# Cross-attention kernel on one core: the mask moved into the score product, and exp and clip over three score banks instead of two

## The chip, the cores and the metric

The kernel runs on one core of one Trainium2 chip. The metric is device time in microseconds from one launch; of three runs before the change the median is 766.37 us (765.65 to 770.05). Five engines work side by side and meet at semaphores: PE (TensorE, matmuls), ACT (ScalarE, activations), DVE (VectorE), POOL (GpSimd) and SP (SyncE, which here only issues DMAs).

## The reference, cut to what matters

Two blocks run one after the other over x (4 batches of 256 rows of 256) with a context of 1601 rows per batch. Block one is a one-head attention and a mixture of 16 experts. Block two is a 16-head attention over the same context, a layer norm of its result, and a second mixture of experts. The change concerns the 16-head attention (head size 16):

```
q, k, v = proj(hs, Wq, bq), proj(at, Wk, bk), proj(at, Wv, bv)
scores = clip(einsum('bhsd,bhtd->bhst', q, k) / 4, -50, 50)
scores = where(attend, scores, -10000.0)
scores = clip(scores, -50.0, 50.0)
probs  = softmax(scores, axis=-1)
probs  = probs / (probs.sum(axis=-1, keepdims=True) + 1e-08)
ctx    = einsum('bhst,bhtd->bhsd', probs, v)
```

A masked key has the score -50, so its weight is exp(-50) and not zero.

## The kernel before, in words

The program is one long hand-ordered instruction stream for each engine. Its parts in time are: block one's attention with the key and value projections of block two beside it (to about 200 us of the profile), the first mixture of experts (to about 430 us), the second attention (434.8 to 660.9 us), and the second mixture of experts with the routing. Only the second attention and the lines that prepare it are touched.

**Jobs and units.** The second attention has 16 jobs (`NJ`): 4 batches times 4 groups of 4 heads. A job has 13 key tiles (`MT`) of 128 keys, the last with 65. One key tile of one job is a unit, numbered x = 0 to 207 (`NALL`).

**Scores (`qk`, line 958).** A head's query and key have 16 numbers each. They are split in a high and a low part, and stand as 48 rows (`KR`): keys high, low, high against queries high, high, low. Two heads lie above each other in the partitions, at rows 0 to 47 (t = 0) and 64 to 111 (t = 1), so that a matmul of one and a matmul of the other use different row halves of the PE array. A unit has four such matmuls of 256 columns, (c, t) = (0,0), (0,1), (1,0), (1,1); the two of one t go to one PSUM bank of 512 columns. So a unit fills two banks, and six banks hold three units (`RING`).

**Exp (line 1438), on ACT.** One activation over the two banks of a unit, 1024 columns, into one of six buffers of `p32` (`PBUF`). The mask comes in as a bias: `kbias`, one number per key, which is a partition here, -1e30 for a masked key and 0 otherwise. Since keys are partitions and each unit has other keys, a bias column belongs to one unit only.

**Clip (line 1946), on DVE.** Clamps the 1024 columns between exp(-50) and exp(50) in place.

**Values (`pv`, line 1000).** For each of the 4 heads of the unit, a matmul with the 17 columns of values and a one (the softmax sum) as weights and 256 columns of `p32` in full fp32, which the profile shows as two MATMULs each. The four heads write to four column groups of the array. They accumulate over the job's 13 units in bank 6 or 7.

**Order on PE.** Line 1079: units go in pairs. First `qk(x)` and `qk(x+1)`, then for each of the two what else is due at that number (`early`: query projections and transposes for later batches; `between`: the output projection, the transposes and router logits of the batch before; `flip`: two transposes of a finished job's result), and then `pv(x-4)` and `pv(x-3)` (`PV_LAG` 4). `qk(x)` waits for `p_exp` of unit x-3, `pv(x)` for `p_clip` of unit x, exp of unit x for `pv_done` of unit x-6.

**Order on ACT and DVE.** Unit by unit, with the small work of `early` and `between` after the exp or clip of its number. On DVE, `evac(job-1)` (a copy of a finished job's result) comes after clip m = 3 and `norm(job-1)` after clip m = 5 of the next job; `flip` on PE is at m = 7 and waits for `evac`.

**SP.** `keys(job)` brings a job's keys to one of three slots of `kst` with six DMAs of 16 partitions. The first three jobs' keys and batch 0's values are asked for in a row; a later job's when the job three before it is scored.

Of the kernel before, what the change touches and what calls it, by code (L numbers as in the profile page):

```python
# [23 lines left out]
P = 128  # L24
# [31 lines left out]
KR = 3 * HD  # L56
PBUF = 6
RING = 3
KSL = 3
PV_LAG = 4  # L60
# [16 lines left out]
def build(nc, a, out, stop="D"):  # L77
    kh_d = nc.dram_tensor("k_hi", [NB * D, MP], F32).ap()
    kl_d = nc.dram_tensor("k_lo", [NB * D, MP], F32).ap()
    v_d = nc.dram_tensor("v_one", [NB, P, MT * NH * VW], F32).ap()  # L80
# [5 lines left out]
    with ExitStack() as ctx:  # L86
# [18 lines left out]
        keep = sb("keep", [P, NB * MT], I32)  # L105
        kbias = sb("kbias", [P, NB * MT])
# [27 lines left out]
        with ExitStack() as s:  # L134
# [20 lines left out]
            Bt("gap3b", [P, 2032])  # L155
# [6 lines left out]
        with ExitStack() as s:  # L162
            C = lambda name, shape, dt=F32: sbuf(s, name, shape, dt)
            qst = C("qst", [P, NB, NH // 2, SEQ], F32R)
            p32 = C("p32", [P, PBUF, 1024])
# [91 lines left out]
        keep_in, kbias_rdy = sem("keep_in"), sem("kbias_rdy")  # L257
# [40 lines left out]
        def at(x):  # L298

            return x // MT, x % MT  # L300

# [68 lines left out]
        def _(sp):  # L370
# [69 lines left out]
            sp.dma_start(keep[:], a["keep"]).then_inc(keep_in, 16)  # L440
# [33 lines left out]
            for t, s in ((wq_raw[:], a["wqT"].rearrange("(k p) n -> p k n", p=P)), (bq[:], a["bq"]),  # L474
# [4 lines left out]
                         (rs[:], a["rs"].rearrange("(o n) -> o n", o=1).broadcast_to([P, 1])), (bq0[:], a["bq0"])):  # L479
# [19 lines left out]

# [23 lines left out]

            for g in range(1, NG - 1):
                queries(0, g)
            for job in range(KSL, NJ):
                sp.wait_ge(sc_rdy, (job - KSL + 1) * MT)
# [133 lines left out]
        def _(pe):  # L661
# [244 lines left out]
            pe.wait_ge(cw_rdy, 6)  # L906
# [29 lines left out]
            def qk(x):  # L936

                job, m = at(x)
                b, g = job // NG, job % NG
                if m == 0:  # L940
                    pe.wait_ge(k_in[job % KSL], 96 * (job // KSL + 1))
                    if b == 0 and g == 0:
                        pe.wait_ge(q_lo, 4)
                    elif b == 0:
                        pe.wait_ge(q_in[g], 16 * 3 * HG)
                    elif b == 1 and g == 0:
                        pe.wait_ge(q_lo, 10)
                    elif b == 2 and g == 0:
                        pe.wait_ge(q_in[NG], 16 * 3 * HG * NG)
                if x >= RING:  # L950
                    pe.wait_ge(p_exp, x - RING + 1)
                elif x == 1:
                    pe.wait_ge(add_rdy, 4)
                rows = rows_of(m)
                for c in range(2):
                    for t in range(2):
                        r = slice(64 * t, 64 * t + KR)
                        mm = pe.matmul(ps[0:rows, 2 * (x % RING) + t, c * SEQ:(c + 1) * SEQ], kst[r, job % KSL, c, m * P:m * P + rows],  # L958
                                       qst[r, b, 2 * g + c, :], start=True, stop=True, skip_group_check=True)
# [25 lines left out]
            def pv(x):  # L985
# [9 lines left out]
                pe.wait_ge(p_clip, x + 1)  # L995
                rows = rows_of(m)
                for j in range(HG):
                    at_ = (m * NH + g * HG + j) * VW
                    c, t = j // 2, j % 2
                    mm = pe.matmul(ps[32 * j:32 * j + VW, 6 + job % 2, 0:SEQ], vsl[0:rows, b % 2, at_:at_ + VW],  # L1000
                                   p32[0:rows, x % PBUF, (2 * t + c) * SEQ:(2 * t + c + 1) * SEQ], start=m == 0, stop=m == MT - 1, skip_group_check=True)
# [76 lines left out]

            for x in range(0, NALL + PV_LAG, 2):
                for y in (x, x + 1):  # L1080
                    if y < NALL:
                        qk(y)
                for y in (x, x + 1):
# [4 lines left out]
                    if y >= PV_LAG:  # L1088
                        pv(y - PV_LAG)
# [1253 lines left out]
```

## Time and profile before

| | us |
|---|---|
| runs (three) | 765.65, 766.37, 770.05 |
| median | 766.37 |
| span of the profiled execution | 765.5 |
| second attention in it (434.8 to 660.9) | 226.1 |
| PE / ACT / DVE busy in the whole span | 702.9 / 396.4 / 537.3 |

The profiled execution's span of 765.5 us lies 0.2 us below the fastest run and 0.9 us below the median; the profile gives no other time for it. Busy PE in this profile counts modelled ends of overlapped matmuls, so 97% busy doesn't say that PE has no room. What it does is better read from the starts of its groups of matmuls: from the start of one group to the start of the next.

### The profile page before, as it was taken

The page shows a single profiled execution, that of the slowest core. Times are in us where ns is not written, and L with a number is a line of the kernel's source. Part 1 is how long each engine was busy: PE and PEld are TensorE (multiplying, and loading weights), DVE is VectorE, ACT ScalarE, POOL GpSimd, SP SyncE. Part 2 cuts the span into 40 slices and gives each one's busy share as a digit, 9 for nine tenths or more (in the row PEclk, how much of TensorE's full clock was granted, in tenths as well). Part 3 has the DMA queues.
Part 4 walks back from the last instruction along what each step waited for, and adds up shares of the span by engine and source line. Part 5 has one row for each costly group of instructions (what it writes and reads, how often), then busy time and mean ns, then how long its engine had stood idle before and what let it go on. Part 6 is the DMA issues. An engine that isn't in the chain of part 4 may idle for free.

```text
span 765.5 us, 14907 instructions
## 1 busy us (share of the span) xinstructions
PE 702.9 (92%) x5499; PEld 531.4 (69%) x5499; DVE 537.3 (70%) x1174; ACT 396.4 (52%) x564; POOL 174.1 (23%) x220
## 2 busy tenths in 40 slices
PE   4899989899899999999999699999999999998990
PEld 3688878798677888888888554455455454577880
DVE  6766566657486666666667788789888878776665
ACT  2633223243322323232322599999999999533550
POOL 5461514421001000000000050002302603532551
PEclk9999999999999999999999899999999999899996
DMA  7456375642625767776778949996969840464545
GB/s 245 132 172 232 122 263 175 221 166 87 186 78 195 248 209 235 253 234 206 237 253 136 192 74 142 209 136 102 210 109 186 128 71 2 133 268 126 166 127 191
DMA packets 55212, 131.16 MB, mean 171 GB/s; under 512 B 12160, under 2 KB 29952, under 8 KB 51568
## 3 DMA queue, kind: packets, MB, share of 16 engines
q1 hardware_dynamic: 51888, 122.93, 60.5%
q0 software_dynamic: 2256, 6.18, 2.4%
q10 hardware_dynamic: 1008, 1.25, 0.5%
q8 instruction: 38, 0.62, 0.4%
q14 instruction: 22, 0.18, 0.1%
HBM read 78.78 MB, written 48.79 MB: 167 GB/s over the span
## 4 chain that ended last, share of the span: by engine, by line
PE 55%; ACT 12%; issue 11%; DVE 9%; DMA 7%; POOL 4%; SPq 1%; DVEq 0%; POOLq 0%; ACTq 0%
PE ps L656 12%; PE ps L657 12%; PE ps L658 12%; ACT p L1438 8%; PE ps L1000 5%; PE ps L958 4%; PE ps L1188 4%; DMA raw<-in_ctxT 2%; PE ps L1204 2%; POOL cTl L612 2%; DMA raw<-in_ctxN 2%; DMA k_lo<-kl 1%; PE ps L1022 1%; ACT cNh L1267 1%; POOL cNl L599 1%
## 5 line engine op out<-in xcount | busy, mean ns | idle before, releaser
L1438 ACT ACTIVATE p<-ps,kbias 128x1024 f32<-128x1024 f32 (+1 forms) x208 | 211.3, 1163 | 5.2 <-PE ps L958 5.0
L1946 DVE TENSOR_SCALAR p<-p 128x1024 f32<-128x1024 f32 (+1 forms) x208 | 140.9, 689 | 26.1 <-ACT p L1438 24.5
L1000 PE MATMUL ps<-p,vsl 128*17 128x256 f32 (+1 forms) x1664 | 113.9, 383 | 2.0 <-DVE p L1946 1.0
L1343 ACT ACTIVATE hh<-h 128x512 fp32r<-128x512 f32 x50 | 31.6, 632 | 132.9 <-DVE h L1813 115.9
L958 PEld LDWEIGHTS ps<-qst,kst 48*128 48x128 f32 (+1 forms) x832 | 58.6, 182 | 60.2 <-ACT p L1438 32.7
L958 PE MATMUL ps<-qst,kst 48*128 48x256 f32 (+1 forms) x832 | 91.1, 318 | 5.5 <-ACT p L1438 1.5
L359 POOL TENSOR_SCALAR nv<-mv 128x2 f32<-128x2 f32 x8 | 6.2, 774 | 359.6 <-DVE mv L1876 211.8
L656 PE MATMUL ps<-xTh,w_hi 128*128 128x512 f32 x200 | 79.8, 399 | 1.5 <-DVE h L1809 0.8
L657 PE MATMUL ps<-xTl,w_hi 128*128 128x512 f32 x200 | 79.2, 396 | 0.0
L658 PE MATMUL ps<-xTh,w_lo 128*128 128x512 f32 x200 | 78.9, 394 | 0.0
L1000 PEld LDWEIGHTS ps<-p,vsl 128*17 128x17 f32 (+1 forms) x1664 | 35.9, 96 | 39.6 <-issue 7.1
L1815 DVE TENSOR_TENSOR hl<-h,hh 128x512 fp32r<-128x512 f32 x50 | 34.6, 692 | 36.6 <-ACT hh L1343 36.6
L656 PE MATMUL ps<-w_hi,hh 128*128 128x256 f32 x200 | 56.9, 284 | 2.1 <-DVE hl L1815 2.0
L1809 DVE TENSOR_TENSOR h<-silu,ps 128x512 f32<-128x512 f32 x50 | 34.4, 689 | 33.5 <-PE ps L658 22.4
L658 PE MATMUL ps<-w_hi,hl 128*128 128x256 f32 x200 | 56.6, 283 | 0.0
L657 PE MATMUL ps<-w_lo,hh 128*128 128x256 f32 x200 | 56.6, 283 | 0.0
L599 POOL TENSOR_TENSOR cNl<-raw,cNh 128x1024 fp32r<-128x1024 f32 (+1 forms) x16 | 31.4, 1983 | 78.1 <-ACT cNh L1267 78.1
L656 PEld LDWEIGHTS ps<-xTh,w_hi 128*128 128x128 f32 x200 | 37.7, 189 | 9.8 <-DVE h L1809 1.7
L658 PEld LDWEIGHTS ps<-xTh,w_lo 128*128 128x128 f32 x200 | 37.5, 187 | 9.0
L657 PEld LDWEIGHTS ps<-xTl,w_hi 128*128 128x128 f32 x200 | 37.8, 189 | 6.5
L656 PEld LDWEIGHTS ps<-w_hi,hh 128*128 128x128 f32 x200 | 38.1, 191 | 6.0 <-DVE hl L1815 4.0
L1339 ACT ACTIVATE silu<-ps 128x512 f32<-128x512 f32 x50 | 29.9, 597 | 19.9 <-PE ps L658 19.0
(308 smaller groups left out, 1551.3 us busy)
## 6 DMA issues: line engine op xcount, KB each, us to landing
x_slots<-blank SPq DMA_DIRECT2D x20, 1032.0 KB, 5.9
kst<-k_hi SPq DMA_DIRECT2D x64, 200.2 KB, 9.1
w_raw<-in_w SPq DMA_DIRECT2D x25, 384.0 KB, 3.5
v_one<-vst SPq DMA_DIRECT2D x4, 1768.0 KB, 8.9
vsl<-v_one SPq DMA_DIRECT2D x4, 1768.0 KB, 17.4
kst<-k_lo SPq DMA_DIRECT2D x32, 200.2 KB, 8.8
raw<-in_ctxN SPq DMA_DIRECT2D x12, 512.0 KB, 5.7
k_hi<-kh SPq DMA_DIRECT2D x24, 256.0 KB, 2.6
```

The costliest lines, as they stand in the source:

```text
L599: pool.tensor_tensor(cNl[:, c0:c0 + w, :], src, cNh[:, c0:c0 + w, :].bitcast(F32), ALU.subtract).then_inc(ctx_split, 1)
L656: e.matmul(o, lh, rh, start=first, stop=False, skip_group_check=True)
L657: e.matmul(o, lh, rl, start=False, stop=False, skip_group_check=True)
L658: return e.matmul(o, ll, rh, start=False, stop=last, skip_group_check=True)
L958: mm = pe.matmul(ps[0:rows, 2 * (x % RING) + t, c * SEQ:(c + 1) * SEQ], kst[r, job % KSL, c, m * P:m * P + rows], qst[r, b, 2 * g + c, :], ...
L1000: mm = pe.matmul(ps[32 * j:32 * j + VW, 6 + job % 2, 0:SEQ], vsl[0:rows, b % 2, at_:at_ + VW], p32[0:rows, x % PBUF, (2 * t + c) * SEQ:(2 ...
L1188: mm = pe.matmul(ps[:, 2 + j % 2, 0:2 * P], xbT[:, j % 2, k * P:(k + 1) * P], weights_of(j, slice(k * 2 * P, (k + 1) * 2 * P)), start=k == ...
L1343: act.activation(hh[:, half, :], h32[:, half, :], ACT.Copy).then_inc(hh_rdy, 1)
L1438: act.activation(p32[0:rows, x % PBUF, :], psf[0:rows, bank * 512:bank * 512 + 1024], ACT.Exp, scale=0.25, bias=kbias[0:rows, col:col + 1] ...
L1809: dve.tensor_tensor(h32[:, half, :], silu[:, half, :], ps[:, 5, :], ALU.mult).then_inc(mul1_rdy, 1)
L1815: dve.tensor_tensor(hl[:, half, :], h32[:, half, :], hh[:, half, :].bitcast(F32), ALU.subtract).then_inc(hl_rdy, 1)
L1946: dve.tensor_scalar(t, t, CLO, CHI, ALU.max, ALU.min).then_inc(p_clip, 1)
```

## The change

It does five things.

1. **Mask.** `keep`, `kbias` and the bias of the exp go. A 49th row joins the score product: in `kst` it holds 0 or -2^100 for each key (`bar_rows`, made by one DVE instruction and sent through DRAM), in `qst` it holds 1. The ones come from spare columns of the weights `wgh`/`wgl` (zeroed) and of the bias `bq0` for the queries that are computed in place, and from six DMAs for the others. `keys(job)` issues eight DMAs instead of six.
2. **Groups.** The 416 banks of scores (2 for each of 208 units) are taken three at a time, over the borders of units and jobs: 139 groups (`NGRP`), the last with two banks. Six banks of PSUM are two slots. `p32` has four buffers of 1536 columns, as many bytes as before.
3. **Exp and clip** are one instruction for each group, over 1536 columns and all 128 partitions, without a bias pointer.
4. **Order of the score product.** The six matmuls of a group go in the order (bank, c) = (0,0), (1,0), (2,0), (1,1), (0,1), (2,1). Banks 0 and 2 of a group have the same t.
5. **Order on PE.** One group of scores, then all other work due, then the values of the units that end in the group three before (`PV_LAG` 3): by turns two units and one.

```diff
-KR = 3 * HD
-PBUF = 6
-RING = 3
+KR = 3 * HD + 1
+BAR = -2.0 ** 100
+PBUF = 4
+GB = 3
+NBANK = 2 * NALL
+NGRP = -(-NBANK // GB)
 KSL = 3
-PV_LAG = 4
+PV_LAG = 3
...
+        def group_of(x):
+            return (2 * x + 1) // GB
+        def units_of(g):
+            return range(-(-(GB * g - 1) // 2), min((GB * g + GB - 2) // 2 + 1, NALL)) if 0 <= g < NGRP else range(0)
+        def width_of(g):
+            return 512 * min(GB, NBANK - GB * g)
...
             load_rest(FFN["B"])
+            sp.wait_ge(bar_rdy, 1)
+            sp.dma_start(bar_d, bar_f).then_inc(row_out, 16)
             scratch_out()
+            sp.wait_ge(row_out, 16)
...
+                    at_ = 64 * t + KR - 1
+                    sp.dma_start(kst[at_:at_ + 1, job % KSL, :, :].bitcast(F32), bar_d[job // NG:job // NG + 1, :].unsqueeze(1).broadcast_to([1, 2, MP])).then_inc(k_in[job % KSL], 16)
...
+            sp.wait_ge(q_hi, 1)
+            sp.wait_ge(tri_rdy, 1)
+            for t in range(2):
+                row = slice(64 * t + KR - 1, 64 * t + KR)
+                every = qst[row, :, :, :].rearrange("o b h (i n) -> o (b h i) n", n=P)
+                per = NH // 2 * SEQ // P
+                for lo, hi in ((4, per), (per + 4, 2 * per), (2 * per, NB * per)):
+                    sp.dma_start(every[:, lo:hi, :].bitcast(F32), ones[0:1, :].bitcast(F32).unsqueeze(1).broadcast_to([1, hi - lo, P])).then_inc(row_out, 16)
...
+            def qk(k):
+                banks = range(GB * k, min(GB * k + GB, NBANK))
+                for n in banks:
+                    if n % (2 * MT) == 0:
+                        first_of(n // (2 * MT))
+                if k >= 2:
+                    pe.wait_ge(p_exp, k - 1)
+                else:
+                    pe.wait_ge(add_rdy, 3 + k)
+                for i, c in ((0, 0), (1, 0), (2, 0), (1, 1), (0, 1), (2, 1)):
+                    if i < len(banks):
+                        x, t = banks[i] // 2, banks[i] % 2
+                        job, m = at(x)
+                        rows = rows_of(m)
                         r = slice(64 * t, 64 * t + KR)
...
-                pe.wait_ge(p_clip, x + 1)
+                pe.wait_ge(p_clip, group_of(x) + 1)
...
-            for x in range(0, NALL + PV_LAG, 2):
-                for y in (x, x + 1):
-                    if y < NALL:
-                        qk(y)
-                for y in (x, x + 1):
+            for k in range(NGRP + PV_LAG):
+                if k < NGRP:
+                    qk(k)
+                for y in units_of(k):
                     early(y)
                     between(y)
                     if y >= MT + FLIP_AT and (y - FLIP_AT) % MT == 0:
                         flip((y - FLIP_AT) // MT - 1)
-                    if y >= PV_LAG:
-                        pv(y - PV_LAG)
+                for y in units_of(k - PV_LAG):
+                    pv(y)
...
-            for x in range(NALL):
-                job, m = at(x)
-                rows, col = rows_of(m), job // NG * MT + m
-                act.wait_ge(sc_rdy, x + 1)
-                if x >= PBUF:
-                    act.wait_ge(pv_done, x - PBUF + 1)
-                bank = 2 * (x % RING)
-                act.activation(p32[0:rows, x % PBUF, :], psf[0:rows, bank * 512:bank * 512 + 1024], ACT.Exp,
-                               scale=0.25, bias=kbias[0:rows, col:col + 1]).then_inc(p_exp, 1)
+            for k in range(NGRP):
+                w = width_of(k)
+                act.wait_ge(sc_rdy, k + 1)
+                if k >= PBUF:
+                    act.wait_ge(pv_done, (GB * (k - PBUF) + GB - 1) // 2 + 1)
+                at_s = k % 2 * GB * 512
+                act.activation(p32[:, k % PBUF, 0:w], psf[:, at_s:at_s + w], ACT.Exp, scale=0.25).then_inc(p_exp, 1)
...
-            def clip(x):
-                t = p32[0:rows_of(x % MT), x % PBUF, :]
-                dve.wait_ge(p_exp, x + 1)
+            def clip(k):
+                t = p32[:, k % PBUF, 0:width_of(k)]
+                dve.wait_ge(p_exp, k + 1)
                 dve.tensor_scalar(t, t, CLO, CHI, ALU.max, ALU.min).then_inc(p_clip, 1)
```

The written order on PE, at a place in the middle where one `flip` falls due. In the names, `qst,kst` is a score product, `p,vsl` a value product, `ident,oS` a flip. Before (line 958 is `qk`, 1000 `pv`, 1008 `flip`):

```order
L958 MATMUL ps<-qst,kst 128x256 [waits p_exp]
L958 MATMUL ps<-qst,kst 128x256 x3
L958 MATMUL ps<-qst,kst 128x256 [waits p_exp]
L958 MATMUL ps<-qst,kst 128x256 x3
L1000 MATMUL ps<-p,vsl 17x256 [waits p_clip]
L1000 MATMUL ps<-p,vsl 17x256 x3
L1008 MATMUL ps<-ident,oS 128x128 [waits oS_rdy]
L1008 MATMUL ps<-ident,oS 128x128
L1000 MATMUL ps<-p,vsl 17x256 [waits p_clip]
L1000 MATMUL ps<-p,vsl 17x256 x3
```

And now (995 is `qk`, 1038 `pv`, 1046 `flip`):

```order
L995 MATMUL ps<-qst,kst 128x256 [waits p_exp]
L995 MATMUL ps<-qst,kst 128x256 x5
L1046 MATMUL ps<-ident,oS 128x128 [waits oS_rdy]
L1046 MATMUL ps<-ident,oS 128x128
L1038 MATMUL ps<-p,vsl 17x256 [waits p_clip]
L1038 MATMUL ps<-p,vsl 17x256 x3
L995 MATMUL ps<-qst,kst 128x256 [waits p_exp]
L995 MATMUL ps<-qst,kst 128x256 x5
L1038 MATMUL ps<-p,vsl 17x256 [waits p_clip]
L1038 MATMUL ps<-p,vsl 17x256 x3
L1038 MATMUL ps<-p,vsl 17x256 [waits p_clip]
L1038 MATMUL ps<-p,vsl 17x256 x3
```

Eight score matmuls between two stretches of values became six, and PE changes between scores and values once for 1.5 units instead of once for 2. On ACT, a stretch before, in the middle of the stage:

```order
L1438 ACTIVATE p<-ps,kbias 128x1024 [waits pv_done,sc_rdy] x12
L1438 ACTIVATE p<-ps,kbias 65x1024 [waits pv_done,sc_rdy]
L1438 ACTIVATE p<-ps,kbias 128x1024 [waits pv_done,sc_rdy] x12
L1418 ACTIVATE xTh<-ps 128x2x256 [waits ln_T]
L1438 ACTIVATE p<-ps,kbias 65x1024 [waits pv_done,sc_rdy]
```

And now:

```order
L1473 ACTIVATE p<-ps 128x1536 [waits pv_done,sc_rdy] x25
L1454 ACTIVATE xTh<-ps 128x2x256 [waits ln_T]
L1473 ACTIVATE p<-ps 128x1536 [waits pv_done,sc_rdy] x9
L1450 ACTIVATE wq_raw<-ps 128x512 [waits dl_rdy,cT_rdy]
```

The other work on ACT is the same; the exps are fewer and wider, without `kbias`.

## Rows read from the trace of the kernel before

**Rows 1.** Busy time by stretch; the fourth is the second attention
```profile
core 0: us, PE busy (x) PEld busy (x) DVE busy (x) ACT busy (x) POOL busy (x), PEclk, DMA share, GB/s
434.80:660.90 226.10, 219.00 (x2649) 114.89 (x2649) 188.00 (x402) 218.73 (x224) 55.07 (x119) 0.99 0.71 120
```

**Rows 2.** Waits in 434.8 to 660.9: who for whom, us, times, longest
```profile
PEld ps L958 <- ACT p L1438: 32.7, 92, 0.5
DVE p L1946 <- ACT p L1438: 24.5, 65, 1.8
PEld ps L1000 <- DVE p L1946: 6.3, 21, 0.9
ACT p L1438 <- PE ps L958: 5.0, 11, 1.0
```

**Rows 3.** Timeline of ACT, 563.4 to 600: start us, length us, instructions merged
```profile
577.65 23.15 ACT L1438 ACTIVATE p<-ps,kbias 128x1024 f32<-128x1024 f32 x23 [0.61 <-PE ps L958]
```

**Rows 4.** Groups of ACT, whole span: count | busy us, mean ns | idle before
```profile
L1438 ACT ACTIVATE p<-ps,kbias 128x1024 f32<-128x1024 f32 (+1 forms) x208 | 211.3, 1163 | 5.2 <-PE ps L958 5.0
L1339 ACT ACTIVATE silu<-ps 128x512 f32<-128x512 f32 x50 | 29.9, 597 | 19.9 <-PE ps L658 19.0
L1479 ACT ACTIVATE sb_<-ps 128x128 f32<-128x128 f32 x31 | 8.6, 278 | 15.7 <-PE ps L1188 15.7
```

**Rows 5.** Timeline of ACT, 24 to 27: with (kh) and without (pTh) a bias
```profile
25.02 1.25 ACT L1258 ACTIVATE kh<-ps,bk 128x512 fp32r<-128x512 f32 x2
26.16 0.59 ACT L1275 ACTIVATE pTh<-ps 128x512 fp32r<-128x512 f32 x1
26.64 1.06 ACT L1267 ACTIVATE cNh<-raw 128x1024 fp32r<-128x1024 f32 x1
```

**Rows 6.** Timeline of PE, 563.4 to 573.6: scores, values, a flip, output projection
```profile
563.79 0.74 PE L958 MATMUL ps<-qst,kst 48*128 48x256 f32 x8
564.46 1.06 PE L1000 MATMUL ps<-p,vsl 128*17 128x256 f32 x16
565.45 0.80 PE L958 MATMUL ps<-qst,kst 48*128 48x256 f32 x8
...
570.18 0.44 PE L1008 MATMUL ps<-ident,oS 128*128 128x128 f32 x2
570.55 1.06 PE L1000 MATMUL ps<-p,vsl 128*17 128x256 f32 x16
...
572.21 0.63 PE L1000 MATMUL ps<-p,vsl 128*17 128x256 f32 x8
572.76 1.13 PE L1022 MATMUL ps<-wo_raw,wq_raw 128*128 128x256 f32 x4
```

**Rows 7.** Timeline of PE, 559.5 to 563.5: four transposes, then values
```profile
562.21 0.66 PE L1015 MATMUL ps<-ident,cx 128*128 128x128 f32 x4
562.80 1.06 PE L1000 MATMUL ps<-p,vsl 128*17 128x256 f32 x16
```

**Rows 8.** Timeline of PE, 421.8 to 423.2: matmuls of 256 columns in line
```profile
421.84 0.28 PE L656 MATMUL ps<-w_hi,hh 128*128 128x256 f32 x1
...
423.15 0.28 PE L658 MATMUL ps<-w_hi,hl 128*128 128x256 f32 x1
```

**Rows 9.** Timeline, 576.8 to 578.9: an exp's end and the clip it releases
```profile
575.94 1.10 ACT L1438 ACTIVATE p<-ps,kbias 65x1024 f32<-65x1024 f32 x1
...
577.08 0.69 DVE L1946 TENSOR_SCALAR p<-p 65x1024 f32<-65x1024 f32 x1 [0.31 <-ACT p L1438]
```

**Rows 10.** The clips, 434.8 to 660.9: ns min/median/max, first and last start
```profile
L1946 DVE TENSOR_SCALAR p<-p x208: 659/692/721, 436.6 to 658.9; 128x1024 f32<-128x1024 f32 x96, 65x1024 f32<-65x1024 f32 x8
```

**Rows 11.** Timeline of SP, 405 to 460: last issue for job 2, first after it
```profile
416.28 0.42 SPq L497 DMA_DIRECT2D kst<-k_hi  x1
439.14 5.21 SPq L510 DMA_DIRECT2D qst<-qh  x8
```

**Rows 12.** DMA issues: KB each, median us from issue to landing
```profile
kst<-k_hi SPq DMA_DIRECT2D x64, 200.2 KB, 9.1
```

More of the change, by code:

```diff
@@ L164, in build @@
             qst = C("qst", [P, NB, NH // 2, SEQ], F32R)
-            p32 = C("p32", [P, PBUF, 1024])
+            p32 = C("p32", [P, PBUF, GB * 512])
             qh, ql = C("qh", [P, KT, NT * P], F32R), C("ql", [P, KT, NT * P], F32R)
@@ L526, in _ @@
             for job in range(KSL, NJ):
-                sp.wait_ge(sc_rdy, (job - KSL + 1) * MT)
+                sp.wait_ge(sc_rdy, group_of((job - KSL + 1) * MT - 1) + 1)
                 keys(job)
@@ L934, in early, with first_of @@
                     queries(3, 7)
-            def qk(x):
-                job, m = at(x)
+            def first_of(job):
                 b, g = job // NG, job % NG
[L940 to L956, printed above, removed]
+                pe.wait_ge(k_in[job % KSL], 128 * (job // KSL + 1))
+                if b == 0 and g == 0:
+                    pe.wait_ge(q_lo, 4)
+                elif b == 0:
+                    pe.wait_ge(q_in[g], 16 * 3 * HG)
+                elif b == 1 and g == 0:
+                    pe.wait_ge(q_lo, 10)
+                elif b == 2 and g == 0:
+                    pe.wait_ge(q_in[NG], 16 * 3 * HG * NG)
+                if job == 1:
+                    pe.wait_ge(row_out, 16 + 96)
@@ L957, in qk @@
                         r = slice(64 * t, 64 * t + KR)
-                        mm = pe.matmul(ps[0:rows, 2 * (x % RING) + t, c * SEQ:(c + 1) * SEQ], kst[r, job % KSL, c, m * P:m * P + rows],
-                                       qst[r, b, 2 * g + c, :], start=True, stop=True, skip_group_check=True)
+                        mm = pe.matmul(ps[0:rows, banks[i] % (2 * GB), c * SEQ:(c + 1) * SEQ], kst[r, job % KSL, c, m * P:m * P + rows],
+                                       qst[r, job // NG, 2 * (job % NG) + c, :], start=True, stop=True, skip_group_check=True)
@@ L998, in pv @@
                     at_ = (m * NH + g * HG + j) * VW
-                    c, t = j // 2, j % 2
+                    c, n = j // 2, 2 * x + j % 2
+                    at_p = n % GB * 512 + c * SEQ
                     mm = pe.matmul(ps[32 * j:32 * j + VW, 6 + job % 2, 0:SEQ], vsl[0:rows, b % 2, at_:at_ + VW],
-                                   p32[0:rows, x % PBUF, (2 * t + c) * SEQ:(2 * t + c + 1) * SEQ], start=m == 0, stop=m == MT - 1, skip_group_check=True)
+                                   p32[0:rows, n // GB % PBUF, at_p:at_p + SEQ], start=m == 0, stop=m == MT - 1, skip_group_check=True)
                 mm.then_inc(pv_done, 1)
@@ L2140, in between @@
                         take_both(t0, t1)
-            for x in range(NALL):
-                clip(x)
-                job, m = at(x)
-                if job and m == EVAC_AT:
-                    evac(job - 1)
-                if job and m == NORM_AT:
-                    norm(job - 1)
-                if m == 8 and job < NT:
-                    dve.tensor_tensor(resid[:, job, :], resid[:, job, :], bet[:], ALU.add).then_inc(beta_rdy, 1)
-                if job == 1 and m == 10:
-                    router_weights()
-                early(x)
-                if 66 <= x < 74:
-                    (shared_hi if x < 70 else shared_lo)(x - 64)
-                between(x)
+            for k in range(NGRP):
+                clip(k)
+                for x in units_of(k):
+                    job, m = at(x)
+                    if job and m == EVAC_AT:
+                        evac(job - 1)
+                    if job and m == NORM_AT:
+                        norm(job - 1)
+                    if m == 8 and job < NT:
+                        dve.tensor_tensor(resid[:, job, :], resid[:, job, :], bet[:], ALU.add).then_inc(beta_rdy, 1)
+                    if job == 1 and m == 10:
+                        router_weights()
+                    early(x)
+                    if 66 <= x < 74:
+                        (shared_hi if x < 70 else shared_lo)(x - 64)
+                    between(x)
             evac(NJ - 1)
```

38 lines of the change are left out of this document (20 added, 18 removed).

## The prediction, made before the result was known

> **What bounds the kernel now.** I read the table by stretch first: the second attention lasts 226.1 us, with ACT busy for 218.7 of them, PE for 219.0 and DVE for 188.0 [rows 1]. Two engines look full, so the waits decide. PE waits for an exp 92 times, 32.7 us in all, while the exps wait for PE 5.0 us in 11 times [rows 2]: ACT rules and PE has room. How much room must come from the starts of PE's groups of matmuls, since its busy time counts overlap twice over.
>
> ACT's price: 23 exps in line took 23.15 us; less the last one's own 1.15, that is 22 steps of **1.00 us** [rows 3]. 208 of them are 208 us. ACT's other work in the stage is its busy 218.7 [rows 1] less the exps' 211.3 [rows 4], 7.4, call it 8 with what overlapped. 216 of 226 are filled.
>
> PE's price, from start to start: two units of scores 0.67 us, two units of values 0.99, one unit of values 0.55, a flip 0.37 [rows 6], a block of four transposes 0.59 [rows 7]. The score blocks come to 104 x 0.67 = 69.7, the values to 104 x 0.99 = 103. The rest: 15 flips x 0.37 = 5.5; 8 blocks of transposes x 0.59 = 4.7; the output projection, 6 calls of four matmuls of 256 columns each, about 1.06 each by the length of its row = 6.4 [rows 6]; the query projections and logits, 24 matmuls of 512 columns at twice 0.12 = 5.8, 12 of 256 at 0.12 = 1.4 and 24 short ones at 0.11 = 2.7, by the step of [rows 8]; the ranks and slower first microseconds, 2.5. That is 29. Together **202 us of 226**: some 24 us of room.
>
> **The change, part by part.**
>
> *Exp.* Without a bias pointer the next instruction starts 0.48 us after one of 512 columns (26.16 to 26.64); with one, 1.25 - 0.68 = 0.57 after it [rows 5]. A column costs (597 - 278)/384 = 0.83 ns [rows 4]; check: 0.57 + 512 x 0.83 ns = 1.00, the exp's step. So a group of 1536 without bias steps at 0.48 + 1024 x 0.83 ns = 1.33 us, against 1.50 for the same columns before. ACT's exps come to 138 x 1.33 + 0.9 = 184.4 us: **23.6 us less work on ACT**, of which 69 fewer instructions at 0.14 make 10 and the missing bias pointer the rest. If the mask's bias were replaced by another pointer nothing but the 10 would be left.
>
> *Clip.* 139 of at most 1.5 x 0.69 = 1.04 us against 208 of 0.69 [rows 10]: no more work than before. DVE is at 188 of 226 and isn't the bound.
>
> *Scores on PE.* This is where I expect the gain to go. Matmuls of 256 columns in one line start every 1.31/11 = 0.12 us [rows 8]. A block of eight takes 0.67; eight in one line would take 0.95, so the two row halves do run beside each other, four in each, 4 x 0.12 = 0.48 plus 0.19 for going in and out. The new block has six matmuls, but banks 0 and 2 have the same t: by the order in the code the halves are used as t, t', t, t', t, t. That is again **four in one half**, 0.67 us for 1.5 units where it was 0.67 for 2. Bounds: 0.55 if the last two were hidden beside something, 6 x 0.12 + 0.19 = 0.91 if the halves stopped overlapping. I take 0.66, near the row of four in line. 139 x 0.66 = 91.7: **22 us more work on PE**. The 49th row makes no matmul longer: 128 rows step at 0.12 [rows 8] as 48 do in the block, (0.67 - 0.19)/4.
>
> *Values.* The same matmuls, in 69 stretches of two units (0.99) and 70 of one (0.54): 68.3 + 37.8 = 106.1, 3 us more, because PE goes over from scores to values 139 times instead of 104. The trace has this price as the 0.1 by which a last step before a change is longer (0.99 is 4 x 0.22 + 0.11). The Trainium skill (TensorEngine Tiling (Array Packing), section Key Properties) says that a change of tiling mode, not of tile, drains the engine, and gives no price; it is the rule that speaks against smaller blocks. Without it, at streams alone (139 x 0.48 + 208 x 0.44 + 29 = 187), PE would stay out of the way.
>
> *The sum on PE.* 91.7 + 106.1 + 29 = 226.8, and 0.7 at the end for the last result's copy: **227.5 us, against 226.1 for the stage before**. ACT would need 184.4 + 8 = 192. So PE takes over as the bound, at the old length.
>
> *Waits that ACT's rule had hidden.* Values waited 6.3 us for clips [rows 2]; a PE without room pays such waits: +2 to +4. The flip: `evac` follows the clip of group_of(13j+3), the flip comes at group_of(13j+7), two or three groups on. With two (5 jobs of 16), the flip is reached about 3.5 us after that group's scores started, and the copy is done at 0.8 + 1.5 + 1.0 + 0.4 = 3.7 to 4.0: up to 0.5 x 5 = 2.2. I take 4 for both.
>
> *Preparation.* One DMA of the old mask goes. SP gets a DMA of the bar rows and a wait for it, two DMAs more for each job, and six for the ones. SP's queue is idle from 416.7 to 439.1 [rows 11], and the keys are asked for two to three jobs ahead while landing takes 9 us [rows 12]; job 0's last key rows land in front of 14 us of idle queue. The two memsets and the bar row's instruction on DVE fall into the first mixture of experts, and no row here prices them: nothing to 1.5 us, I take 0; the cover would be gone only if the queue ran 10 us late.
>
> The sum: 227.5 + 4 = 231.5 for the stage, +5.4. On the profiled execution's 765.5 that gives 770.9; the median of the runs lies 0.9 above that execution, so 771.8. I say **771.5**.
>
> **The rivals.**
>
> *A: the gain arrives.* If PE's last two score matmuls cost less than a full step each (0.55 a block), PE has 139 x 0.11 = 15.3 less: 212, and the stage, with 4 of waits, 216: 10 us less, **756.5**. At its best ACT stays the ruler at 192 + 10 of stalls as before = 202: 741.4. For it: ACT was the ruler, and each of its gains is certain. Against it: the count of four in one half, and no row shows a step under 0.11. By the Trainium skill (ScalarE: Activation LUTs, section What ACT_TABLE_LOAD costs) a pointer operand adds about 93 ns to an ACTIVATE and back-to-back ones overlap by as much, which is what [rows 4, 5] show; by that page alone one would expect the whole 23.6 (742). Chance of more than 1% faster: 0.16.
>
> *B: a ring through exp and values (slower).* `p32` has four buffers, and for even groups k exp k waits for the values of the unit that straddles groups k-4 and k-3; PE does that unit after scores k. And scores k+2 wait for exp k. So each even group passes a ring: scores 0.66, first unit of values to its last end 0.62 (as the stretch of one unit at 572.21 [rows 6]), exp 0.597 + 1024 x 0.83 ns = 1.45 [rows 4], and two handovers between engines at 0.04 (577.04 to 577.08 [rows 9]): 2.81 us for three units. PE's own round is 2 x 0.66 + 0.99 + 0.54 = 2.85. The ring decides from 0.04 us more on: an exp that costs as much as with a pointer (+0.09), or a handover of 0.1. At 0.2 beyond PE's round it costs 69 x 0.2 = 14 us on top of the forecast: **785**. For it: the closeness, and that flips and transposes now stand between scores and values, inside the ring. Against it: such work lengthens PE's round by the same amount. Chance of a result over 1% slower, this and more exposed waits together: 0.31, of which the ring 0.2.
>
> *C: the halves stop overlapping.* 0.91 a block: 139 x 0.25 = 35 us, **806**. Nothing in the rows speaks for it but the odd order; 0.03 more.
>
> *The forecast,* PE as the ruler and a time within 1%: 0.50. About 7.7 us either way is what a measurement of this kernel can tell from no change, so the borders are 758.7 and 774.0; my forecast is inside but near the upper one.
>
> **The numbers.** Forecast 771.5. Its own range, by 0.62 to 0.70 a block and 2 to 7 us of waits, is 763 to 779. To hold 8 in 10 it reaches to A's first value and to B: **755 to 785**. Faster 0.16, same 0.50, slower 0.34.
>
> **What the new profile would show.** ACT's exps at 1.33 us when in line, and mostly not in line: exps that wait for PE rise from 5 us to 25 or more, and PE's waits for exps fall from 32.7 to under 8. Score blocks of six start to start at 0.66; 0.55 would prove A, 0.9 C. The ring would show as exps of even groups that start right after a value product's end and score blocks that wait for them, by turns. DVE's clips near 0.95 to 1.0. The prediction is wrong if PE still waits for exps for over 15 us, or if the stage lasts under 220 or over 240.

## The result, and the profile after

The changed kernel takes **782.32 us** (median of four runs, 780.8 to 784.35), the kernel before 766.01 beside it: ratio **1.021**, 95% interval 1.018 to 1.024. It is slower by 16 us. A second set of runs gave 783.24 against 768.15, ratio 1.021 (1.016 to 1.025). The times are medians of all executions, but the ratios leave out single ones that were slower at a lower granted clock, above all one of 892.61 us at 0.741 in the run with the later flip, whose median without it is 779.7. The forecast was 771.5 and no change within 1%; the range of 755 to 785 holds the time, the forecast's own range of 763 to 779 doesn't, and the direction was wrong.

The table by stretch, of the kernel after. The first line is the second attention, now 241.7 us; it answers to the first of [rows 1]. The other two are stretches inside it, and the last three columns are granted clock, DMA share and GB/s.

```profile
core 0: us, PE busy (x) PEld busy (x) DVE busy (x) ACT busy (x) POOL busy (x), PEclk, DMA share, GB/s
435.90:677.60 241.70, 234.02 (x2651) 129.25 (x2651) 181.22 (x333) 202.58 (x155) 56.37 (x119) 0.98 0.67 116
...
556.00:576.00 20.00, 20.00 (x224) 11.48 (x220) 13.19 (x27) 16.11 (x13) 0.00 (x0) 0.91 0.87 155
...
596.00:636.00 40.00, 39.34 (x456) 21.62 (x449) 29.76 (x63) 33.57 (x26) 15.30 (x27) 0.96 0.76 143
```

ACT is busy for 203 of 242 us, where it was busy for 218.7 of 226.1: it did get the room it was promised, and the stage became 15.5 us longer all the same. PE is busy nearly throughout. So the time is PE's, or is lost between PE and the others. The work ahead of this stage took 1.1 us more (it starts at 435.98, where it started at 434.85), the work behind it 0.8 us less.

The page's groups of exp and clip, after (busy, mean ns of one, then idle before them and what ended it), to be set against [rows 4, 10]:

```profile
L1473 ACT ACTIVATE p<-ps 128x1536 f32<-128x1536 f32 (+1 forms) x139 | 194.3, 1448 | 36.9 <-PE ps L1038 28.4
L1982 DVE TENSOR_SCALAR p<-p 128x1536 f32<-128x1536 f32 (+1 forms) x139 | 131.9, 955 | 49.0 <-ACT p L1473 48.3
```

1448 ns for an exp and 955 for a clip are the forecast's 1.45 and 0.95 to 1.0. The waits of the stage, after (total, times, longest), against [rows 2]:

```profile
PEld ps L995 <- ACT p L1473: 37.8, 82, 0.8
ACT p L1473 <- PE ps L1038: 28.4, 32, 2.6
...
ACT p L1473 <- PE ps L995: 4.4, 3, 2.7
PEld ps L1046 <- DVE oS L1988: 3.7, 6, 1.0
PEld ps L1038 <- DVE p L1982: 3.4, 12, 0.7
```

The exps wait for PE, 32.8 us in all, most of it for **values** (L1038), not for scores (L995). And the weight loads of the scores still wait for exps, 82 times. Each waits for the other: that is a ring, which the forecast had priced and put second.

One turn of it, on PE and then on ACT, after:

```profile
486.15 0.73 PE L995 MATMUL ps<-qst,kst 49*128 49x256 f32 x6
486.81 1.06 PE L1038 MATMUL ps<-p,vsl 128*17 128x256 f32 x16
487.81 0.73 PE L995 MATMUL ps<-qst,kst 49*128 49x256 f32 x6
488.46 0.63 PE L1038 MATMUL ps<-p,vsl 128*17 128x256 f32 x8
489.08 0.39 PE L995 MATMUL ps<-qst,kst 49*128 49x256 f32 x2
```

```profile
487.57 1.46 ACT L1473 ACTIVATE p<-ps 128x1536 f32<-128x1536 f32 x1
```

The block of scores that starts at 486.15 belongs to an even group. Its exp may not overwrite its buffer of `p32` before the first of the two units that start at 486.81 is done. With 0.62 for a unit up to its last end that is 487.43; the exp starts at 487.57, ends at 489.03, and the scores two groups on start at 489.08. The turn is 0.66 + 0.62 + 0.14 + 1.46 + 0.05 = **2.93 us**. PE alone would need 0.66 + 0.99 + 0.66 + 0.56 = 2.87. The stretch of one unit lasts from 488.46 to 489.08, 0.62, though it needs 0.56: those 0.04 to 0.06 us are the whole loss in a turn. Of 68 such stretches in the stage 23 take 0.56 us, 35 take 0.60 to 0.62, and 10 take more (up to 0.89).

### The profile page after: what moved, and what is told of

Its sections match the earlier page's. It is cut to its first block, busy times and chain, and to the rows that moved or that the text cites. A ratio compares the mean times of both kernels' runs of the same rounds, so it can differ in the third digit from the quotient of the medians.

```text
span 781.4 us, 14741 instructions
## 1 busy us (share of the span) xinstructions
PE 715.3 (92%) x5499; PEld 543.8 (70%) x5499; DVE 531.3 (68%) x1107; ACT 380.1 (49%) x495; POOL 174.7 (22%) x220
## 3 DMA queue, kind: packets, MB, share of 16 engines
q10 hardware_dynamic: 1008, 1.25, 0.5%
## 4 chain that ended last, share of the span: by engine, by line
PE 61%; DVE 12%; DMA 8%; POOL 7%; ACT 7%; issue 4%; SPq 1%; DVEq 0%; POOLq 0%; ACTq 0%
PE ps L684 11%; PE ps L686 11%; PE ps L685 11%; PE ps L1038 9%; PE ps L995 8%; PE ps L1225 4%; ACT p L1473 2%; DMA raw<-in_ctxT 2%; DMA raw<-in_ctxN 2%; PE ps L1241 2%; POOL cTl L640 2%; DMA k_lo<-kl 2%; POOL cNl L627 1%; DVE p L1982 1%; PE ps L1060 1%
## 5 line engine op out<-in xcount | busy, mean ns | idle before, releaser
L1473 ACT ACTIVATE p<-ps 128x1536 f32<-128x1536 f32 (+1 forms) x139 | 194.3, 1448 | 36.9 <-PE ps L1038 28.4
L1982 DVE TENSOR_SCALAR p<-p 128x1536 f32<-128x1536 f32 (+1 forms) x139 | 131.9, 955 | 49.0 <-ACT p L1473 48.3
L1038 PE MATMUL ps<-p,vsl 128*17 128x256 f32 (+1 forms) x1664 | 118.1, 388 | 2.7 <-issue 2.5
L995 PEld LDWEIGHTS ps<-qst,kst 49*128 49x128 f32 (+1 forms) x832 | 73.3, 184 | 63.9 <-ACT p L1473 37.8
L995 PE MATMUL ps<-qst,kst 49*128 49x256 f32 (+1 forms) x832 | 102.3, 314 | 2.2 <-issue 1.1
L1038 PEld LDWEIGHTS ps<-p,vsl 128*17 128x17 f32 (+1 forms) x1664 | 35.1, 97 | 38.3 <-issue 8.5
L684 PEld LDWEIGHTS ps<-xTh,w_hi 128*128 128x128 f32 x200 | 37.8, 189 | 9.4 <-DVE h L1845 1.7
L1607 DVE SCALAR_TENSOR_TENSOR kl<-ps,bk,kh 128x512 fp32r<-128x512 f32 (+1 forms) x32 | 19.5, 631 | 30.6 <-ACT kh L1295 30.6
```

Of the source, the lines that this page charges most:

```text
L684: e.matmul(o, lh, rh, start=first, stop=False, skip_group_check=True)
L995: mm = pe.matmul(ps[0:rows, banks[i] % (2 * GB), c * SEQ:(c + 1) * SEQ], kst[r, job % KSL, c, m * P:m * P + rows], qst[r, job // NG, 2 * ( ...
L1473: act.activation(p32[:, k % PBUF, 0:w], psf[:, at_s:at_s + w], ACT.Exp, scale=0.25).then_inc(p_exp, 1)
L1982: dve.tensor_scalar(t, t, CLO, CHI, ALU.max, ALU.min).then_inc(p_clip, 1)
```

## The experiments

All were timed in five rounds beside the kernel before. A difference between two of them is a difference of their ratios times 766, and is known to 3 or 4 us either way. I held three theories: that PE's own work is what grew (fuller half 4 of 6, and more changes between scores and values); that the ring decides; and that the mask row, its pointer or its preparation had a part.

One thing isn't the same in all of them. Inside the second attention TensorE's granted clock was at half for 3.4 us in the profile of the kernel before and for 10.2 in that of the changed kernel. In the profiles of the experiments, in the order below, it was 4.8, 3.4, 14.7, 6.8, 10.2, 3.4, 17.1 and 10.2 us, and 6.8 in the changed kernel's second. PE at work loses half of such a time at most. So up to 5 us of a difference between two profiled stages can be the clock's, and no difference below is corrected for it.

### The mask row without the groups of three

The kernel before, in its order and its two-bank exps, with the 49th row and no bias pointer:

```diff
-KR = 3 * HD
+KR = 3 * HD + 1
...
-                act.activation(p32[0:rows, x % PBUF, :], psf[0:rows, bank * 512:bank * 512 + 1024], ACT.Exp,
-                               scale=0.25, bias=kbias[0:rows, col:col + 1]).then_inc(p_exp, 1)
+                act.activation(p32[0:rows, x % PBUF, :], psf[0:rows, bank * 512:bank * 512 + 1024], ACT.Exp, scale=0.25).then_inc(p_exp, 1)
```

> The kernel before with the mask as a 49th row and an exp without bias pointer, but still two banks (1024 columns) an exp and a clip, three slots, and the old order on PE. Theory (three banks a group cost PE four score matmuls in one half and more changes of mode, the missing pointer is the whole gain): PE's blocks stay 0.67 for two units of scores and 0.99 for two of values, PE needs 203 us as before; the exps step at 0.57 - 0.09 + 512 x 0.83 ns = 0.91 instead of 1.00, ACT needs 208 x 0.91 + 8 = 197; the stage falls from 226 to 208 to 215, the median to 748 to 756. Rival (the row itself, its DMAs and the ones are what made the change slow): 766 or more.

Measured: **761.48 us**, ratio 0.993 (0.990 to 0.996). It is faster than both kernels, by less than expected; its stage took 219.8 us against 226.1. Its waits:

```profile
PEld ps L974 <- ACT p L1453: 19.7, 47, 0.4
...
PEld ps L1016 <- DVE p L1961: 12.2, 24, 2.0
...
ACT p L1453 <- PE ps L974: 9.8, 16, 1.0
```

Values waited 12.2 us for clips, against 6.3 before [rows 2]. With ACT out of the way DVE's bursts of small work came to the surface. I take it that they took most of the gain that was missing; no run shows that by itself. The groups of three with all that goes with them (wider exp and clip, four buffers, the order inside the block and on PE), then, cost 761.5 to 782.3, **21 us**.

### The same with a pointer to zeros

```diff
-                act.activation(p32[0:rows, x % PBUF, :], psf[0:rows, bank * 512:bank * 512 + 1024], ACT.Exp, scale=0.25).then_inc(p_exp, 1)
+                act.activation(p32[0:rows, x % PBUF, :], psf[0:rows, bank * 512:bank * 512 + 1024], ACT.Exp,
+                               scale=0.25, bias=zero[0:rows, 0:1].bitcast(F32)).then_inc(p_exp, 1)
```

> As the one before, but the exp gets a bias pointer to a column of zeros. Theory: the exps step at 1.00 again, ACT rules, 765 to 769. If the row and its preparation cost anything, it stands here alone, beyond 769. If the pointer has no price in line, this equals the kernel without it.

Measured: **768.18**, ratio 1.003 (1.001 to 1.005), as expected. This kernel does what the kernel before does except for where the mask comes from, so the row with its preparation costs about 2 us (0.5 to 4). The profiles place none of it in the stage: the stage took 226.5 us in both kernels from the first scores to the last flip's end, and started 1.0 us earlier here. The exp's row of the two profiles, without and with the pointer:

```profile
L1453 ACT ACTIVATE p<-ps 128x1024 f32<-128x1024 f32 (+1 forms) x208 | 193.3, 1051 | 10.0 <-PE ps L974 9.8
```

```profile
L1453 ACT ACTIVATE p<-ps,zero 128x1024 f32<-128x1024 f32 (+1 forms) x208 | 211.1, 1158 | 5.2 <-PE ps L974 5.2
```

107 ns an exp by the mean, 17.8 us of ACT's busy time in all, of which the kernel's time got back some 8 (1.003 to 0.993).

### Changing between scores and values at every unit

The first experiment's kernel, with scores and values taking turns at every unit instead of every two:

```diff
-            for x in range(0, NALL + PV_LAG, 2):
-                for y in (x, x + 1):
+            for x in range(0, NALL + PV_LAG):
+                for y in (x,):
```

> The kernel with the mask row and two banks an exp (761.5), with PE going over between scores and values for every unit, 208 times instead of 104. Theory (going in and out of a score block costs 0.19, leaving values another 0.1): a unit takes 0.44 + 0.55 = 0.99 instead of 0.83, PE needs 208 x 0.99 + 29 = 235 instead of 203; ACT needs 197; the stage goes from 220 to 236 to 242, the median to 778 to 784. If a change of mode is free and only matmuls count: 761 to 764.

Measured: **781.31**, ratio 1.019 (1.016 to 1.022): 20 us slower, with every instruction the same. PE of the kernel in pairs, then of this one:

```profile
600.95 0.93 PE L974 MATMUL ps<-qst,kst 49*128 49x256 f32 x8
601.81 1.06 PE L1016 MATMUL ps<-p,vsl 128*17 128x256 f32 x16
```

```profile
601.39 0.63 PE L1016 MATMUL ps<-p,vsl 128*17 128x256 f32 x8
601.95 0.50 PE L974 MATMUL ps<-qst,kst 49*128 49x256 f32 x4
602.38 0.63 PE L1016 MATMUL ps<-p,vsl 128*17 128x256 f32 x8
```

A unit takes 0.43 + 0.56 = 0.99 from start to start (601.39 to 602.38), where half a pair takes (0.67 + 0.99)/2 = 0.83 (0.67 for most blocks; the one shown, 0.86, is of the slower ones). A block of scores is 0.12 a step of the fuller half plus 0.19, one of values 0.22 a step plus 0.11, so **each turn from scores to values and back costs 0.30 us**. 104 turns more make 31 us; 20 arrived, since the kernel in pairs had room on PE. Up to 5 of the 23 us by which the profiled stage grew can be the clock (14.7 us at half against 4.8). 0.99 a unit is longer than ACT's 0.91, and 182 of 205 blocks of scores take 0.43 or 0.44 and 199 of 204 of values 0.55 or 0.56: PE decides here by its work alone, with no ring.

### One score matmul less in each group

The changed kernel without the sixth matmul of each group: half of one bank in three, a sixth of the scores, isn't computed; exp and clip are as they were.

```diff
-                for i, c in ((0, 0), (1, 0), (2, 0), (1, 1), (0, 1), (2, 1)):
+                for i, c in ((0, 0), (1, 0), (2, 0), (1, 1), (0, 1)):
```

> The changed kernel without the last score matmul of each group (columns 256 to 511 of the third bank are not computed; only its time is of use): three in one half instead of four, five in all. Theory with the ring (scores k, first unit of values, exp k, scores k+2 for even k, 2.92 us a round of three units as the trace shows): the ring holds one block of the two, so 69 x 0.11 = 7.6 us less, 774 to 776. Theory without the ring (PE alone rules, 139 blocks): 15 us less, 766 to 768. If the count in one half didn't matter but only the change of mode: no difference, 781 to 783.

Measured: **775.66**, ratio 1.010 (1.007 to 1.014): 8 us less than the changed kernel. Three matmuls in the fuller half instead of four take PE 139 x 0.11 = 15 us of work off. Half of it arrived. PE, from its profile:

```profile
487.57 0.62 PE L995 MATMUL ps<-qst,kst 49*128 49x256 f32 x5
488.12 0.63 PE L1038 MATMUL ps<-p,vsl 128*17 128x256 f32 x8
488.85 0.62 PE L995 MATMUL ps<-qst,kst 49*128 49x256 f32 x5
489.39 1.06 PE L1038 MATMUL ps<-p,vsl 128*17 128x256 f32 x16
490.38 0.62 PE L995 MATMUL ps<-qst,kst 49*128 49x256 f32 x5
```

The block takes 0.55 (487.57 to 488.12), and the stretch of one unit behind it has grown from 0.56 to 0.73 (488.12 to 488.85). A turn is 2.81 (487.57 to 490.38) against 2.93: only the one block that lies inside the ring shortened it, and the other's 0.11 went into the wait. By the ring's own sum it is 2.93 - 0.11 = 2.82. So the ring holds as soon as PE's work is shorter.

### Breaking the ring

The unit that straddles two groups gets its values one iteration earlier, so that an even group's exp finds its buffer free:

```diff
+            def values_at(k):
+                mine, nxt = list(units_of(k - PV_LAG)), list(units_of(k - PV_LAG + 1))
+                if len(mine) == 2 and k > PV_LAG:
+                    mine = mine[1:]
+                if len(nxt) == 2:
+                    mine = mine + nxt[:1]
+                return mine
...
-                for y in units_of(k - PV_LAG):
+                for y in values_at(k):
```

> The changed kernel, with the values of the unit that straddles two groups done one iteration earlier (two units in odd iterations, one in even), so that exp k never waits for values that come after scores k. Ring theory: the round falls from 2.92 to PE's own 2.86, 69 x 0.06 = 4 us less, plus up to 3 where other work stood in the ring; 775 to 779. If PE alone rules: 781 to 783. If clips now come too late for the earlier values: more than 784.

Measured: **779.31**, ratio 1.017 (1.014 to 1.020), 2.7 us under the changed kernel, just above what was expected. The times alone don't tell this from nothing. The waits and PE's row do:

```profile
ACT p L1481 <- PE ps L995: 27.5, 40, 1.9
...
PEld ps L995 <- ACT p L1481: 8.5, 19, 0.8
PEld ps L1038 <- DVE p L1990: 6.8, 15, 1.1
```

```profile
475.82 0.74 PE L995 MATMUL ps<-qst,kst 49*128 49x256 f32 x6
476.49 0.63 PE L1038 MATMUL ps<-p,vsl 128*17 128x256 f32 x8
477.04 0.74 PE L995 MATMUL ps<-qst,kst 49*128 49x256 f32 x6
477.71 1.06 PE L1038 MATMUL ps<-p,vsl 128*17 128x256 f32 x16
478.70 0.73 PE L995 MATMUL ps<-qst,kst 49*128 49x256 f32 x6
```

A turn is 475.82 to 478.70, 2.88, and 63 of the stretches of one unit now take 0.56. The exps wait for scores (L995) and no longer for values. **29 us of waits of the weight loads went (37.8 to 8.5) and the kernel gained 3**: most of such a wait runs beside the matmuls still in the array, and only the 0.04 to 0.06 us by which the stretch is longer is PE's loss.

### Both at once

> Both edits at once: the straddling unit's values one iteration earlier, and no last score matmul in a group (columns 256 to 511 of the third bank are not computed; only its time is of use). With the ring gone PE alone should rule, so the missing step must now show in all 139 blocks: 15 us below the ring edit alone (779), 762 to 766; while with the ring in place it gave 7 (775.7). If it gives 7 again, something other than PE and the ring holds the round.

Measured: **769.54**, ratio 1.004 (1.002 to 1.007); a sixth of the scores is again not computed. That is 10 us under the kernel with the ring broken, where its block's 15 were expected (762 to 766); up to 3 of the 10 can be the clock. A turn of PE is now 0.55 + 0.55 + 0.55 by these rows (the last block ends at 487.31), and 0.99 for the stretch of two units, 2.64:

```profile
485.66 0.62 PE L995 MATMUL ps<-qst,kst 49*128 49x256 f32 x5
486.21 0.63 PE L1038 MATMUL ps<-p,vsl 128*17 128x256 f32 x8
486.76 0.62 PE L995 MATMUL ps<-qst,kst 49*128 49x256 f32 x5
```

and ACT's two exps in line are 2 x 1.33 = 2.66. The engines have met. What I had missed is that the values' waits for clips come up with it; that they hold the 5 us that didn't arrive is likely, and no run shows it:

```profile
PEld ps L995 <- ACT p L1481: 22.5, 52, 0.6
PEld ps L1038 <- DVE p L1990: 13.1, 26, 1.5
```

### Another order inside the block

The kernel with the ring broken, with the matmuls of bank 0 and 2, which are of one half, first, then those of bank 1:

```diff
-                for i, c in ((0, 0), (1, 0), (2, 0), (1, 1), (0, 1), (2, 1)):
+                for i, c in ((0, 0), (0, 1), (2, 0), (2, 1), (1, 0), (1, 1)):
```

> The ring edit with the six score matmuls in the order t, t, t, t, t', t': the two of the other half come last. Theory (PE issues in order, a half does one at a time, a half's matmul may run beside the other half's last one): five steps in line instead of four, a block of 0.77 instead of 0.66, 139 x 0.11 = 15 us more than 779: 792 to 796. If only the count in the fuller half mattered, whatever the order: 779. If halves didn't overlap in the changed kernel at all, the order is nothing: 779.

Measured: **779.8**, ratio 1.017 (1.014 to 1.020), no other time than its model's. Four of one half and then two of the other take what the mixed order takes:

```profile
486.61 0.74 PE L995 MATMUL ps<-qst,kst 49*128 49x256 f32 x6
487.28 1.07 PE L1038 MATMUL ps<-p,vsl 128*17 128x256 f32 x16
```

My theory that the order decides was wrong. What counts is how many matmuls the fuller half has: four, 0.66 to 0.67. A split of three and three, with one bank filled from both halves, was not tried.

### The flip one unit later

The kernel with the ring broken, with `FLIP_AT` 8 instead of 7.

> The kernel with the values of a straddling unit one iteration earlier (779.31 us), and the transposes of a finished job's result one unit later (FLIP_AT 8 instead of 7). If the five late flips of the changed kernel cost what the profile's wait shows (3.7 us over six, less what an exp or score wait behind them takes back), this is 1.5 to 2.5 us faster than the kernel it is made from: 777 to 778. If that wait only takes the place of another (PE has about 0.1 us of room in a round there), the time stays at 779 to 780. In its trace no transpose at L1046's place waits for the copy of the finished job; the values' waits for clips may grow by up to 1 us.

Measured: **780.55**, ratio 1.018 (1.014 to 1.022), against 1.017 without it. The flips' wait for the copy fell from 3.0 us to 1.0, the kernel's time didn't fall with it: inconclusive between 0 and 2 us, and the expected 777 to 778 wasn't reached. The profiled stage was 3.2 us shorter (236.1 against 239.3, both with 10.2 us at half clock), in an execution that was the fastest of its kernel.

### The changed kernel again

> The changed kernel once more, without an edit. It asks which parts of the 15.5 us that its second attention grew are there in every profile and which are not. If the ring of the score slots is a cause, a second profile has the same periods: value stretches of two units .99 us, of one unit .60 to .61 against .56, exps waiting for PE 26 to 30 us, score blocks waiting for exps 35 to 40 us, five flips late by .35 to .48 us. If the half granted clock at 567.5 and at 629.0 us belongs to the router logits of a batch (12 to 24 matmuls of 16 columns), it stands there again and costs 3 to 4 us; if it is chance, one or both are gone, and the stage is 238 to 240 us instead of 241.6. The time: 780 to 784.

Measured: 783.24, ratio 1.021. What belongs to the order of the work stands there again: the weight loads of the scores wait 38.9 us 84 times, the exps 27.6 us for values, 24 stretches of one unit at 0.56 and 32 at 0.60 to 0.62. The granted clock does not:

```profile
556.00:576.00 20.00, 20.00 (x216) 11.36 (x214) 13.26 (x26) 16.05 (x14) 0.00 (x0) 0.91 1.01 163
...
596.00:636.00 40.00, 39.43 (x471) 22.04 (x475) 30.60 (x66) 34.42 (x27) 15.74 (x29) 1.00 0.80 148
```

The drop near 568 us is there again, the one near 629 isn't.

## Why the prediction was wrong, by its own steps

**Right.** *Exp* and *Clip*: 1448 and 955 ns, as forecast. *Scores on PE*: 110 of 138 blocks take 0.66 or 0.67, the count of four in one half is shown by the run with five matmuls (0.55) and by the one in another order (0.67). *PE takes over*: shown by the first experiment and the one at every unit; groups of three cost PE 139 turns instead of 104, 35 x 0.30 = 10.5 us, and 139 x 4 x 0.12 against 104 x 4 x 0.12 for the fuller half, 16.8 us, together 27, and PE's room was 24. With one block's step less and the ring broken the time is back at 1.004. *The flip*: five flips are late, as forecast, by 0.35 to 0.48 us. One of them starts at 505.36, 1.01 us after the block of scores before it (504.35) instead of 0.66:

```profile
504.35 0.73 PE L995 MATMUL ps<-qst,kst 49*128 49x256 f32 x6
505.36 0.44 PE L1046 MATMUL ps<-ident,oS 128*128 128x128 f32 x2 [0.28 <-DVE oS L1988]
```

*Rival A* (the gain arrives) and *rival C* (0.91 a block) are out: no block took 0.55 with six matmuls (0.58 was the least), none 0.91 as a rule.

**Wrong.** The forecast had the stage at 231.5 us, it took 241.6, from the first scores (435.98) to the last flip (677.6). The 10 us, term by term, from the trace of after, by the starts of PE's rows:

| term | forecast | measured |
|---|---|---|
| scores, 139 x 0.66 (the last group has four matmuls) | 91.7 | 91.5 |
| values, 69 x 0.99 and 70 x 0.54 (0.56) | 106.1 | 107.4 |
| other work of PE | 29 | 29.1 |
| waits for clips and for late copies | 4 | 3.2 |
| the ring: stretches of one unit over 0.56, one late block of scores | 0 | 3.4 |
| the first groups of the stage | 0 | 3.4 |
| half clock inside the stage, behind the start | 0 | 3.0 |
| end | 0.7 | 0.6 |
| sum | 231.5 | 241.6 |

The late copies are those of the five flips, 2.0 us, and of two blocks of transposes (at 612.01 and 671.93), 1.2 us.

No single term made it. Three that the forecast held at nothing made 9.8 us of the 10: **the step that failed is "The sum on PE", which with 4 us for all waits took PE to be a ruler that little holds up; it was held up for 13 us.** Two of the three, the ring and the first groups, are waits of the kind that 24 us of room absorbed before; now there is no room. The clock is another matter: the kernel before had no such drop there that its room could have absorbed. The values' 1.3 us are mis-sized: a stretch of one unit was read as 0.55, taken at 0.54, and measures 0.56.

- *Rival B, the ring.* It does decide, at the point that the prediction named ("a handover of 0.1"), but by some 0.05 a turn, not 0.2. That its 785 lies nearest to the measured 782 is therefore luck in good part: it charged 14 us to the ring, which cost about 3. The mis-sized term is the handover from values to exp: 0.14 us (487.43 to 487.57), priced at 0.04 from that of exp to clip [rows 9]. The exp waits for two semaphores here, its scores and the buffer, but that isn't the price: in the kernel with the ring broken the same exps start 0.04 after the last score matmul in all 38 cases where the scores come last. Where the buffer comes last, in the changed kernel, it is 0.13 in the middle of 32 cases (0.11 at least). The trace shows the wait for the buffer as an instruction of its own on ACT ahead of the exp: in another turn the last value matmul ends at 563.63, that instruction stands at 563.69 and the exp at 563.76. Whether the other order of the two waits would give the 0.09 back was not tried.
- *The first groups.* The first value matmul came 10.06 us after the stage's first scores, at 446.04, where it was 8.24 before (443.09). What it waited for isn't a clip of its own group, which had ended at 439.2. By the code (`free_again`) the first job's values wait until DVE has taken the second query projection out of their bank, and DVE does that behind the clip of the third group (444.32), from 445.20 to 445.94:

```profile
444.32 0.96 DVE L1982 TENSOR_SCALAR p<-p 128x1536 f32<-128x1536 f32 x1 [0.29 <-ACT p L1473]
445.20 0.74 DVE L1932 SCALAR_TENSOR_TENSOR ql<-ps,bq,qh 128x512 fp32r<-128x512 f32 x1
```

```profile
446.04 0.63 PE L1038 MATMUL ps<-p,vsl 128*17 128x256 f32 x8 [2.46 <-issue]
```

  With wider exps and clips in front of it on ACT and DVE this small work comes later. The pauses and slow matmuls around the first four blocks of scores make 3.4 us; around the first three blocks of the kernel before they made 2.1, which the forecast had not counted either. So 3.4 us of the miss, but only 1.3 of the change, are these.
- *The clock.* The granted clock was at 1.2 GHz, half, for 3.4 us at 567.5 and at 629.0, where before there was no such stretch between 440.3 and 662.1. At each a step of values takes 0.43 instead of 0.22, and by the starts of the rows 1.5 and 1.4 us were lost. PE had no pause there. At 567.5 it had just come through twelve matmuls of 16 columns, the router logits (the last is shown):

```profile
567.18 0.26 PE L686 MATMUL ps<-gwh_d,xTl 128*128 128x16 f32 x1
567.36 1.81 PE L1038 MATMUL ps<-p,vsl 128*17 128x256 f32 x16
```

  At 629.0 such matmuls had ended 1.6 us earlier, with values, scores and transposes between. The Trainium skill (TensorE: Matmul & The Clock Gate, Part 1) says that activity opens the clock and idling closes it, at two levels; the levels agree with this trace, and the drop here came with PE at work. The second profile had one of the two drops, and its stage was 1.0 us shorter. Of the other five kernels with groups of three, three had neither drop and two had the second alone, there within 0.4 us behind the same matmuls. So four of the five drops stand right behind them, and most such places have none. So this term is shown as a loss in each profile, and isn't shown as a fixed price of the change. It isn't the profile's alone: over all executions on record the middle value of the mean granted clock is 0.980 for the kernel before (50 of them) and 0.9725 for the changed one (10). That is some 6 us of the 16 at most, an estimate by (1 - clock) times the time, and how much of it PE paid isn't shown. The kernel before issues the same short matmuls without such a drop, and why they come now is open.

**What the profile would show**, as far as not told: "waits for exps under 8 us" failed outright, with 37.8. But of those, only about 3 were PE's, as the run without the ring showed. The view named in the prediction couldn't tell the two, because the profile books the wait on the weight load while PE finishes its last matmuls. "The stage under 220 or over 240" did say wrong, rightly.

Open remain what lowers the clock, how much of the 16 us it is from one execution to the next, and whether the preparation or the row itself makes the 2 us of the second experiment.

## What to carry to other kernels

Count turns, not only matmuls: every change between two kinds of matmul that share the array differently has its price (0.30 us there and back here), and a block whose halves are filled four to two costs what four and four cost. When a change takes work from the ruling engine and gives it to the next, compare the sum with that engine's room (27 us added against 24), and expect that the small things the old wait absorbed (a late copy, a slow handover, a slow start) now show in the time. The half of this change that only took work away from ACT was worth having: the mask row with the old pairs gives 761.5 us, 0.7% better than the kernel before and 2.7% better than the changed one.

## What the runs showed of the hardware that was not expected

- The order of matmuls over two row halves doesn't matter inside a block of six (0.66 mixed, 0.67 one half first); the fuller half's count does.
- A wait on a weight load of 0.46 us on average (37.8 us in 82) cost the matmuls behind it some 0.04 to 0.06.
- From the last value matmul to the exp that it releases 0.13 us (middle of 32), where the wait stands in an instruction of its own on ACT; from the last score matmul to the same exp 0.04 us (38 of 38), where it doesn't.
- The clock fell to half for 3.4 us while PE was busy, at the same place (right behind twelve short matmuls) in two profiles of one kernel, and at a second place in only one of them.
